# Four-stage transformer block on one core: the projections and the output product of the first stage moved to other slots

## The chip, the cores and the metric

The kernel runs on one core of a Trainium2 chip. The metric is device microseconds of one execution; the lower, the better.

## The reference, cut to what matters

X is 16 sequences of 512 tokens with 256 features, in fp32. Four layers follow each other, each with a layer norm before it and a residual sum behind it:

```python
x = x + attn_a(layernorm(x))     # 16 heads of width 64, exact gelu, output product
x = x + ffn(layernorm(x))        # ternary weights, relu, 256 -> 1024 -> 256
x = x + attn_b(layernorm(x))     # 16 heads of width 16, rotary positions, biases
x = x + ffn(layernorm(x))

def attn_a(X):                   # the first stage, the one that the change touches
    Q, K, V = X @ Wq, X @ Wk, X @ Wv             # 256 -> 1024 each, 16 heads of 64
    attn = softmax(Q K^T / sqrt(64))             # 512 x 512 per head
    A = gelu(attn @ V)                           # exact
    return X + A @ Wpost                         # 1024 -> 256
```

## The kernel before, in words

The program has two stages. The first computes attn_a for all 16 sequences; the second does the other three layers. The change touches the first alone, so only that is told here.

**Units and slots.** A sequence has 16 heads, worked on in 8 pairs. A pair takes 4 units, one for each half of the queries (256 rows) and head; so a sequence has 32 units (`UNITS`) and the stage 512. Every engine walks the same list of *slots*, one for each unit, and in each slot does a fixed set of things, in the order in which its own loop names them. Nothing but semaphores ties the engines together. Slots are counted here from the first of a sequence (slot 0) to 31; slot -1 of a sequence is slot 31 of the one before. In slot u:

- **PE** computes the scores of unit u+3 (`a_scores`, lines L627 and L628, 4 matmuls of 512 columns into half of `ps_s`, which holds two units), then turns the normalised exponentials of unit u (`a_transposes`, L640, two banks of 4 transposes each), then, in every fourth slot (0, 4, 8 and so on: *the values' slots*), the values of the pair that is complete (`a_values`, L656, 32 matmuls), and last the slot's *products* from the table below.
- **ACT** first copies the high part of the products that PE did in the slot before (`a_high`; L837 for q and k), then one turned bank (L824), then takes the exponentials of unit u+3 (L815, two halves, with sums). In slots 19 and 35 (which is slot 3 of the next sequence) it then runs four gelus (L847).
- **DVE** inverts the sums of unit u+2 (L994), then does the low part or copy of the products of the slot before (`a_low`; L1012 for q and k), then the maxima of unit u+3 (L987), then copies the other turned bank (L1001), and behind these the rarer work: the values' copy (L1030, slots 1, 5, 9 ...), the high parts of the gelu results (L1036, slots 4, 5, 20, 21), the statistics (slots 15 to 17) and the normalised rows of the next sequence (`a_normalise`, L982, slots 19 and 20).
- **POOL** multiplies the exponentials of unit u+2 by the inverse of their sums (L535), and computes the low parts of the gelu results (L539).
- **SP** issues the six DMAs that build the stacked q and k of a pair (`a_stack`), in slots -6, -2, 2, 6 and so on; they must have landed before PE computes the first scores of that pair, three slots later.

**Products.** A product is a group of matmuls into one of three PSUM banks: kind "x" is the turned normalised input (two of them, L668), "qk" the projection of a pair to q (i=0) or k (i=1) (six matmuls of 512 columns, L222), "v" the projection of 128 tokens to half of the values (six matmuls, L229), "post" the output product of two blocks of 128 tokens with half of the heads (24 matmuls of 256 columns, L687). They are called Q, V, P and X below.

**Banks.** The two turned banks of each slot and every product are *fills*, numbered in the order of PE's work; fill f goes into bank f mod 3. PE begins a fill only when fill f-3 has been emptied. The first turned bank of a slot is emptied by DVE, the second by ACT; Q and k's product by ACT and then DVE; P by DVE; V by DVE or ACT by the table `value_copy` (of the eight, numbers 0 and 2 of the first half and number 2 of the second go to ACT).

**The tables** that set the slots stand in the lines that the diff shows. Before, the products of pair p stand in slots 4p-8 and 4p-7 (of which the first is a values' slot).

Of the kernel before, what the change touches and what calls it, by code (L numbers as in the profile page):

```python
# [13 lines left out]
def hybrid_block_kernel(nc, X, WQ, WK, WV, WPOST, WB, BQK, BV, WO, BO, W1T, B1, W2T, B2, COS, SIN, X1, OUT):  # L14
# [20 lines left out]
    UNITS = 2 * H  # L35
# [4 lines left out]
    with ctx:  # L40
# [241 lines left out]


        UNITS_ALL = BATCH * UNITS
        XT, QK_FIRST, VALUE_SLOTS = -10, -8, ((-6, -5, -2, -1), (3, 3, 7, 15))
        POST = ((27, 31), (42, 43))
        STATS, AGGREGATE, POWER, NORMALISE = (-17, -16), -15, -15, (-13, -12)
        RESIDUAL, LOAD_X, SAVE_X, STACK_FIRST = 13, -20, 44, -6
        GELUS = (19, 35)
# [7 lines left out]
        def late(s, half):  # L297
            return LATE if (s, half) == (BATCH - 1, 1) else 0

        todo_of = {}  # L300
        for s in range(BATCH):
            for k in range(KT):
                todo_of.setdefault(UNITS * s + XT, []).append(("x", k, 0, s))
            for p in range(PAIRS):
                for i in range(2):
                    todo_of.setdefault(UNITS * s + QK_FIRST + 4 * p + i, []).append(("qk", p, i, s))
            for g in range(2):
                for tok in range(TB):
                    todo_of.setdefault(UNITS * s + VALUE_SLOTS[g][tok], []).append(("v", g, tok, s))
            for half in range(2):  # L310
                for two in range(2):
                    todo_of.setdefault(UNITS * s + POST[half][two] + late(s, half), []).append(("post", half, two, s))

# [951 lines left out]
```

## Time and profile before

| | us |
|---|---|
| median of 3 runs | 4111.77 (4111.37 to 4117.78) |
| profiled execution, its own time | 4113.93 |
| its span | 4112.1 |
| PE busy in the span | 3803.7 (92%) |
| DVE busy | 2600.6 (63%) |
| ACT busy | 2378.7 (58%) |
| POOL busy | 1927.9 (47%) |

The span is what the hardware profiler records from the first to the last instruction; 1.8 us lie around it. PE counts matmuls alone; its weight loads run beside them. The first stage's slots with all their work run from 53.7 us (slot 0 of the first sequence) to about 2341 us; the rest is the second stage.

### The profile page before, as it was taken

The page shows a single profiled execution, that of the slowest core. Times are in us where ns is not written, and L with a number is a line of the kernel's source. Part 1 is how long each engine was busy: PE and PEld are TensorE (multiplying, and loading weights), DVE is VectorE, ACT ScalarE, POOL GpSimd, SP SyncE. Part 2 cuts the span into 40 slices and gives each one's busy share as a digit, 9 for nine tenths or more (in the row PEclk, how much of TensorE's full clock was granted, in tenths as well). Part 3 has the DMA queues.
Part 4 walks back from the last instruction along what each step waited for, and adds up shares of the span by engine and source line. Part 5 has one row for each costly group of instructions (what it writes and reads, how often), then busy time and mean ns, then how long its engine had stood idle before and what let it go on. Part 6 is the DMA issues. An engine that isn't in the chain of part 4 may idle for free.

```text
span 4112.1 us, 65455 instructions
## 1 busy us (share of the span) xinstructions
PE 3803.7 (92%) x23682; PEld 2697.8 (66%) x23682; DVE 2600.6 (63%) x4143; ACT 2378.7 (58%) x4593; POOL 1927.9 (47%) x1219
## 2 busy tenths in 40 slices
PE   6999999999999999999999878999999999999987
PEld 4777777777777777777777654555555555555544
DVE  5665666666566666656656656666666666666662
ACT  3565655556565555655656535666666666666654
POOL 2554455555445455544545543444444444444412
PEclk9999999999999999999999978999999999999998
DMA  4444344344344334444434423232222222322220
GB/s 112 93 103 97 84 103 103 80 101 103 88 93 103 92 88 103 95 96 93 99 92 93 112 49 50 51 55 53 52 53 53 54 52 54 55 54 50 50 42 16
DMA packets 152368, 315.59 MB, mean 77 GB/s; under 512 B 23088, under 2 KB 76720, under 8 KB 152048
## 3 DMA queue, kind: packets, MB, share of 16 engines
q1 hardware_dynamic: 152048, 311.39, 35.3%
q8 instruction: 192, 3.15, 0.3%
q14 instruction: 128, 1.05, 0.1%
HBM read 33.43 MB, written 25.17 MB: 14 GB/s over the span
## 4 chain that ended last, share of the span: by engine, by line
PE 55%; DVE 20%; ACT 13%; issue 7%; POOL 3%; DMA 0%; SPq 0%; DVEq 0%; POOLq 0%; ACTq 0%
PE ps_o L656 10%; DVE neg_max L987 7%; ACT e_a L815 5%; PE ps_o L728 5%; PE ps_t L222 4%; DVE max_b L1128 4%; PE ps_t L764 4%; PE ps_s L701 3%; ACT raw_a L837 3%; PE ps_t L687 3%; PE ps_t L229 3%; PE ps_t L755 3%; PE ps_t L640 3%; PE ps_m L222 2%; DVE xn L1106 2%
## 5 line engine op out<-in xcount | busy, mean ns | idle before, releaser
L535 POOL TENSOR_TENSOR e_a<-e_a,recip 128x1024 f32<-128x1024 f32 x512 | 969.5, 1894 | 1045.1 <-DVE recip L994 1045.1
L815 ACT ACTIVATE e_a<-ps_s,neg_max 128x512 f32<-128x512 f32 x1024 | 693.9, 684 | 249.6 <-DVE neg_max L987 238.7
L853 ACT ACTIVATE et<-ps_s 128x1024 f32<-128x1024 f32 x512 | 523.6, 1023 | 432.9 <-PE ps_s L715 432.8
L1128 DVE TENSOR_REDUCE max_b<-ps_s 128x2 f32<-128x1024 f32 x512 | 623.9, 1219 | 209.3 <-PE ps_s L701 208.0
L987 DVE TENSOR_REDUCE neg_max<-ps_s 128x2 f32<-128x1024 f32 x512 | 621.1, 1213 | 25.3 <-PE ps_s L628 25.3
L656 PE MATMUL ps_o<-et_a,v_a 128*64 128x256 f32 x4096 | 470.3, 382 | 0.0
L640 PE MATMUL ps_t<-ident,e_a 128*128 128x128 f32 x2736 | 394.6, 275 | 41.9 <-DVE et_a L1001 35.8
L627 PE MATMUL ps_s<-stack_a 128*128 128x512 f32 x1024 | 413.0, 403 | 12.9 <-DMA stack_a<-raw_a 8.6
L569 POOL TENSOR_TENSOR h_lo<-h,h_hi 128x512 fp32r<-128x512 f32 x256 | 329.2, 1300 | 180.0 <-ACT h_hi L897 180.0
L628 PE MATMUL ps_s<-stack_a 128*128 128x512 f32 x1024 | 402.4, 393 | 0.0
L640 PEld LDWEIGHTS ps_t<-ident,e_a 128*128 128x128 f32 x2736 | 321.2, 141 | 110.7 <-DVE et_a L1001 51.8
L656 PEld LDWEIGHTS ps_o<-et_a,v_a 128*64 128x64 f32 x4096 | 282.7, 137 | 150.8 <-issue 21.3
L824 ACT ACTIVATE et_a<-ps_t 128x512 f32<-128x512 f32 x339 | 202.2, 596 | 297.5 <-PE ps_t L640 297.3
L994 DVE RECIPROCAL recip<-sums 128x2 f32<-128x2 f32 x512 | 84.8, 166 | 401.4 <-ACT e_a L815 401.4
L701 PE MATMUL ps_s<-k_stack,q_stack 48*128 48x512 f32 x1024 | 261.1, 506 | 68.6 <-DVE max_b L1128 68.1
L557 POOL TENSOR_TENSOR rstd<-rstd,minus_half 128x4 f32<-128x4 f32 x48 | 49.3, 1027 | 499.2 <-DVE rstd L1099 497.6
L728 PE MATMUL ps_o<-et,v_b 128*32 128x512 f32 x2048 | 280.4, 620 | 0.0
L1012 DVE SCALAR_TENSOR_TENSOR raw_a<-ps_t,raw_a 128x512 fp32r<-128x512 f32 x171 | 118.3, 692 | 244.1 <-ACT raw_a L837 242.8
L701 PEld LDWEIGHTS ps_s<-k_stack,q_stack 48*128 48x128 f32 x1024 | 98.4, 187 | 217.5 <-issue 121.8
L1001 DVE COPY et_a<-ps_t 128x512 f32<-128x512 f32 x345 | 234.9, 681 | 0.0
L627 PEld LDWEIGHTS ps_s<-stack_a 128*128 128x128 f32 x1024 | 193.1, 189 | 56.4 <-DMA stack_a<-raw_a 11.6
L640 PE MATMUL ps_m<-ident,e_a 128*128 128x128 f32 x1360 | 206.8, 275 | 19.2 <-DVE et_a L1001 16.8
(207 smaller groups left out, 7965.1 us busy)
## 6 DMA issues: line engine op xcount, KB each, us to landing
stack_a<-raw_a SPq DMA_DIRECT2D x256, 384.0 KB, 4.7
stack_a<-raw_a SPq DMA_DIRECT2D x256, 256.0 KB, 4.3
stack_a<-raw_a SPq DMA_DIRECT2D x256, 128.0 KB, 3.6
q_stack<-roped_q SPq DMA_DIRECT2D x256, 64.0 KB
k_stack<-roped_k SPq DMA_DIRECT2D x256, 64.0 KB
x_a<-X SPq DMA_DIRECT2D x16, 512.0 KB, 3.5
X<-x_a SPq DMA_DIRECT2D x16, 512.0 KB, 3.0
x_ahead<-X SPq DMA_DIRECT2D x16, 512.0 KB, 3.8
```

The source lines that it names most:

```text
L535: nc.gpsimd.tensor_tensor(e_a[:, u % 4, :, :], e_a[:, u % 4, :, :], factor, ALU.mult).then_inc(e_normed, 1)
L569: nc.gpsimd.tensor_tensor(h_lo[:, i, :], h32[:, n % 4, :], h_hi[:, i, :], ALU.subtract).then_inc(h_split, 1)
L627: mm(out, st[:, 0, c:c + P], st[:, 1, :], start=True, stop=False)
L628: last = mm(out, st[:, 0, c:c + P], st[:, 2, :], start=False, stop=True)
L640: last = nc.tensor.transpose(bank(fill)[:, c:c + P], e_a[:, u % 4, j, t * P:(t + 1) * P], ident[:, :])
L656: last = mm(ps_o[HA * h:HA * (h + 1), half * HS:(half + 1) * HS], v_a[:, t, c:c + HA], et_a[:, (4 * n + 2 * half + h) % 5, t, :], start=(t ...
L701: last = mm(ps_s[:, score_bank(u) + h, :], q_stack[rows, pair, block_ * P:(block_ + 1) * P], k_stack[rows, pair, :], start=True, stop=True)
L728: last = mm(ps_o[32 * h:32 * (h + 1), :], v_b[:, s % 2, keys, 4 * quad + h, :], et[:, (2 * w + h // 2) % 5, h % 2, :], start=(keys == 0), ...
L815: ins = nc.scalar.activation(e_a[:, u % 4, j, :], ps_s[:, 2 * (u % 2) + j, :], ACT.Exp, bias=neg_max[:, u % 4, j:j + 1], accum_out=sums[:, ...
L853: nc.scalar.activation(et[:, v % 5, :, :], ps_s[:, 2:4, :], ACT.Exp)\
L987: nc.vector.reduce_max(neg_max[:, u % 4, :], ps_s[:, 2 * (u % 2):2 * (u % 2) + 2, :], AX.X, negate=True)\
L1128: nc.vector.reduce_max(max_b[:, u // 4 % 2, :, u % 4], ps_s[:, score_bank(u):score_bank(u) + 2, :], AX.X, negate=True).then_inc(max_done, 1)
```

## The change

Four tables of slots are written anew; the names, the number of products and what each computes stay.

| | before | after |
|---|---|---|
| Q of pair p (i=0, i=1) | 4p-8, 4p-7 | 4p-9, 4p-7 |
| V, first half of the heads | -6, -5, -2, -1 | -7, -5, -1, 2 |
| V, second half | 3, 3, 7, 15 | 2, 6, 14, 18 |
| P, first half of the heads | 27, 31 | 26, 30 |
| P, second half | 42, 43 (10, 11 of the next) | the same |
| X | -10 | the same |

So the products by slot of a sequence in the midst of the stage (slots 24 to 31 hold products of the next one):

| slots | before | after |
|---|---|---|
| 0 to 3 | Q, Q, none, V V | none, Q, V V, Q |
| 4 to 7 | Q, Q, none, V | none, Q, V, Q |
| 8 to 11 | Q, Q, P, P | none, Q, P, P Q |
| 12 to 15 | Q, Q, none, V | none, Q, V, Q |
| 16 to 19 | Q, Q, none, none | none, Q, V, Q |
| 20 to 23 | Q, Q, X X, none | none, Q, X X, Q |
| 24 to 27 | Q, Q, V, P V | none, Q V, P, Q V |
| 28 to 31 | Q, Q, V, P V | none, Q, P, Q V |

```diff
-        XT, QK_FIRST, VALUE_SLOTS = -10, -8, ((-6, -5, -2, -1), (3, 3, 7, 15))
-        POST = ((27, 31), (42, 43))
+        XT, QK_SLOTS, VALUE_SLOTS = -10, (-9, -7), ((-7, -5, -1, 2), (2, 6, 14, 18))
+        POST = ((26, 30), (42, 43))
...
             for p in range(PAIRS):
                 for i in range(2):
-                    todo_of.setdefault(UNITS * s + QK_FIRST + 4 * p + i, []).append(("qk", p, i, s))
+                    todo_of.setdefault(UNITS * s + QK_SLOTS[i] + 4 * p, []).append(("qk", p, i, s))
```

PE's rows of slot 14 and of the first half of slot 15, before (L627 and L628 are the scores, L640 the turned exponentials):

```order
L627 MATMUL ps_s<-stack_a 128x512
L628 MATMUL ps_s<-stack_a 128x512
L627 MATMUL ps_s<-stack_a 128x512
L628 MATMUL ps_s<-stack_a 128x512
L640 MATMUL ps_t<-ident,e_a 128x128 x4
L640 MATMUL ps_m<-ident,e_a 128x128 x4
L627 MATMUL ps_s<-stack_a 128x512
L628 MATMUL ps_s<-stack_a 128x512
L627 MATMUL ps_s<-stack_a 128x512
L628 MATMUL ps_s<-stack_a 128x512
L640 MATMUL ps_t<-ident,e_a 128x128 x8
```

and now:

```order
L627 MATMUL ps_s<-stack_a 128x512
L628 MATMUL ps_s<-stack_a 128x512
L627 MATMUL ps_s<-stack_a 128x512
L628 MATMUL ps_s<-stack_a 128x512
L640 MATMUL ps_t<-ident,e_a 128x128 x8
L229 MATMUL ps_m<-wa_hi,xh_a 128x512
L229 MATMUL ps_m<-wa_lo,xh_a 128x512
L229 MATMUL ps_m<-wa_hi,xh_a 128x512
L229 MATMUL ps_m<-wa_lo,xh_a 128x512
L229 MATMUL ps_m<-wa_hi,xl_a 128x512 x2
L627 MATMUL ps_s<-stack_a 128x512
```

Slot 14, which held no product, has a V now; behind it PE goes on to the scores of slot 15.

ACT's rows around the four gelus of slot 19, before, from the exponentials of slot 19 to those of slot 20 and the copy behind them:

```order
L815 ACTIVATE e_a,sums<-ps_s,neg_max 128x512 x2
L847 ACT_TABLE_LOAD
L847 ACTIVATE heads_a<-heads_a 128x512 x4
L824 ACTIVATE et_a<-ps_m 128x512
L815 ACT_TABLE_LOAD
L815 ACTIVATE e_a,sums<-ps_s,neg_max 128x512 x2
L837 ACTIVATE raw_a<-ps_t 128x512
```

and now:

```order
L815 ACTIVATE e_a,sums<-ps_s,neg_max 128x512 x2
L847 ACT_TABLE_LOAD
L847 ACTIVATE heads_a<-heads_a 128x512 x4
L837 ACTIVATE raw_a<-ps_t 128x512
L824 ACTIVATE et_a<-ps_t 128x512
L815 ACT_TABLE_LOAD
L815 ACTIVATE e_a,sums<-ps_s,neg_max 128x512 x2
```

The high part of a Q (L837) stands right behind the gelus now, ahead of the turned bank and the next exponentials; it stood behind the next exponentials. The same holds around the gelus of slot 3.

## Rows read from the trace of the kernel before

**Rows 1.** The page's first part: busy time of each engine over the span.

```profile
PE 3803.7 (92%) x23682; PEld 2697.8 (66%) x23682; DVE 2600.6 (63%) x4143; ACT 2378.7 (58%) x4593; POOL 1927.9 (47%) x1219
```

**Rows 2.** Windows, each four slots from 0: length, PE, PEld, DVE, ACT, POOL, clock, DMA, GB/s.

```profile
918.08:936.48 18.40, 17.00 (x105) 12.97 (x104) 10.80 (x17) 9.69 (x23) 6.11 (x5) 1.00 0.30 69
936.48:952.47 15.99, 15.35 (x100) 11.91 (x99) 10.69 (x19) 11.71 (x24) 9.93 (x7) 1.00 0.30 64
952.47:972.62 20.15, 19.86 (x142) 16.50 (x140) 11.36 (x19) 10.97 (x27) 10.34 (x7) 1.00 0.55 125
972.62:988.62 16.00, 15.36 (x101) 11.92 (x99) 9.30 (x14) 7.60 (x18) 8.35 (x5) 1.00 0.39 106
988.62:1003.73 15.11, 14.23 (x93) 10.63 (x92) 10.83 (x25) 8.72 (x22) 7.79 (x5) 1.00 0.41 92
1003.73:1022.55 18.82, 15.82 (x101) 11.67 (x101) 14.68 (x26) 14.49 (x30) 12.99 (x8) 1.00 0.47 103
1022.55:1043.09 20.54, 19.96 (x131) 16.03 (x130) 12.24 (x20) 11.57 (x28) 11.15 (x7) 1.00 0.51 115
1043.09:1063.01 19.92, 19.64 (x129) 15.97 (x128) 11.02 (x17) 9.53 (x23) 7.58 (x5) 1.00 0.36 81
```

**Rows 3.** Timeline of PE, slots 0 to 3: start, length, what, [idle before it <- releaser].

```profile
923.57 0.50 PE L222 MATMUL ps_t<-xh_a,wa_hi 128*128 128x512 f32 x1
...
925.06 0.40 PE L627 MATMUL ps_s<-stack_a 128*128 128x512 f32 x1
...
928.23 0.39 PE L627 MATMUL ps_s<-stack_a 128*128 128x512 f32 x1
...
929.94 0.47 PE L627 MATMUL ps_s<-stack_a 128*128 128x512 f32 x1
...
932.19 0.66 PE L640 MATMUL ps_m<-ident,e_a 128*128 128x128 f32 x4 [0.64 <-DVE et_a L1001]
```

**Rows 4.** Timeline of PE in slot 31: a P, begun at the first row, V behind it.

```profile
1058.67 0.36 PE L687 MATMUL ps_t<-wpost_hi,heads_parts 128*128 128x256 f32 x1
...
1061.62 0.40 PE L229 MATMUL ps_m<-wa_hi,xh_a 128*128 128x512 f32 x1
```

**Rows 5.** Timeline of ACT and DVE in slots 1 to 3.

```profile
929.09 0.59 ACT L837 ACTIVATE raw_a<-ps_t 128x512 fp32r<-128x512 f32 x1
...
929.71 0.69 DVE L1012 SCALAR_TENSOR_TENSOR raw_a<-ps_t,raw_a 128x512 fp32r<-128x512 f32 x1 [0.32 <-ACT raw_a L837]
...
930.32 1.22 DVE L987 TENSOR_REDUCE neg_max<-ps_s 128x2 f32<-128x1024 f32 x1
...
931.45 0.68 DVE L1001 COPY et_a<-ps_m 128x512 f32<-128x512 f32 x1
...
933.05 0.17 DVE L994 RECIPROCAL recip<-sums 128x2 f32<-128x2 f32 x1 [0.92 <-ACT e_a L815]
933.13 1.20 DVE L987 TENSOR_REDUCE neg_max<-ps_s 128x2 f32<-128x1024 f32 x1
```

**Rows 6.** Timeline of ACT and DVE around the gelus of slot 19.

```profile
1005.51 0.81 DVE L982 TENSOR_SCALAR xn_a<-x_a,mean_var,rstd 128x256 f32<-128x256 f32 x2
...
1006.28 0.20 ACT L815 ACTIVATION_READ_ACCUMULATOR e_a<-ps_s,neg_max 128x1 f32 x1
1006.50 1.28 ACT L847 ACT_TABLE_LOAD   x1
...
1009.01 1.53 POOL L539 TENSOR_TENSOR heads_parts<-heads_a,heads_parts 128x512 fp32r<-128x512 f32 x1 [0.36 <-DVE heads_parts L1036]
1009.32 1.70 DVE L982 TENSOR_SCALAR xn_a<-x_a,mean_var,rstd 128x256 f32<-128x256 f32 x2
...
1009.89 0.58 ACT L824 ACTIVATE et_a<-ps_m 128x512 f32<-128x512 f32 x1
1010.48 1.28 ACT L815 ACT_TABLE_LOAD   x1
```

**Rows 7.** SP's last DMA of one pair's stack, and time to landing of such DMAs.

```profile
934.82 0.60 SPq L412 DMA_DIRECT2D stack_a<-raw_a  x1
...
DMA to landing us min/median/max: 4.3/4.7/5.9
```

## The prediction

> **What bounds the kernel now.** I read the page first: PE is busy for 92% of the span, the next engine for 63% [rows 1]. That says that the order of PE's work and its holes matter, not where the holes are. So I cut one sequence in the midst of the first stage into its eight groups of four slots [rows 2]. They add up to 144.9 us, at a full clock; I take this sequence for all of the stage. PE is busy in 137.2 of them. The busy time hides part of the loss, since the matmuls' ends are modelled; the timeline tells it better [rows 3, 4]. From scores to scores a slot without a product takes 1.71 us (928.23 to 929.94), one with a Q 3.17 (925.06 to 928.23): a Q is 1.46, and so is a V. A P is 2.95 (1058.67 to 1061.62). A values' slot up to its product is 5.49 (918.08 to 923.57). An X is four transposes, about 0.45. The first scores behind values cost 0.1 more, a second product of a slot 0.06 less. One values' slot and three slots with a Q or V make 15.1; the eight groups with all the products make **133.2 us**. So PE stands still for 11.7 us a sequence, which is what a better order could get back: over some 15.5 sequences (of the last, only the slots up to 22 hold everything) 181 us.
>
> What it stands still for is shown in slot 3 [rows 3]: a turned bank waits for DVE's copy. Behind that is a loop between DVE and ACT [rows 5]. Call M the start of a slot's maxima (930.32). DVE's turned copy begins 1.13 later and is done at M+1.81; PE begins at M+1.87 (932.19). ACT's exponentials end, and the inverse starts, at M+2.73 (933.05); the next maxima at M+2.81 (933.13) when there is nothing to empty. When a Q is to be emptied, ACT's high part starts 0.10 before the inverse could, DVE's low part 0.62 later, the maxima 0.61 behind that: M+3.83. A V emptied by DVE takes M+3.42, one emptied by ACT leaves it at M+2.81. Before, two slots in a row need 3.83 and then comes a slot in which PE has only 1.71 us of work: PE runs into the loop's lag. Maxima also can't start before the slot's scores, 1.1 behind its start (1.2 behind values).
>
> **The change, group by group.** The number of instructions stays but for some that join or part; nothing is added. The sum is a matter of waits alone, so for each group I take the floor from above and add the waits that the loop's times give.
>
> *Slots 12 to 15.* Count from the start of slot 1 of a group (13 here). The values' slot of 5.49 lets the loop catch up, so M=1.20. Its Q is emptied at 1.20+2.60+0.62+0.69 = 5.11. PE reaches the V of the next slot at 3.26+1.71 = 4.97, but that V needs the bank of the Q: it waits until 5.17, 0.2. The V is emptied by ACT, in time. 15.1+0.2 = **15.3**, before 16.0 [rows 2].
>
> *Slots 16 to 19.* The same, but DVE empties the V: M is 5.03, the copy is done at 5.03+2.81+0.69 = 8.53, PE can go on at 8.59, and the Q in slot 19 would start at 8.34: another 0.25. **15.55**, before 15.1, with two products more in it than before (V and the second Q), where slot 20's left.
>
> *Slots 8 to 11, 24 to 27, 28 to 31.* A P is long enough to let the loop catch up; only the wait on the Q stays (none in 24 to 27, where a V stands between). 19.5+0.2, 19.4 and 18.0+0.2: **19.7, 19.4, 18.2**, before 20.15, 20.5, 19.9.
>
> *Slots 0 to 3.* 15.1+1.46 for the second V, 0.2 for the first, and 0.27 for the second, whose bank is slot 2's turned one (M+1.87 = 6.90, PE there at 6.63): **17.0**, before 18.4.
>
> *Slots 4 to 7.* Here the change has a price. The gelus of slot 3 take ACT for 3.4 us (table load at 1006.50, next work at 1009.89 [rows 6]). The high part of slot 3's Q now stands behind them; before, slot 3 had only V's, emptied by DVE. Count from slot 4: exponentials of slot 3 end at 0.64, the high part starts at 4.05, M is 5.28, the load of the exponentials' table (1.28) ends at 6.5, the inverse comes at 8.0, not 4.9. Slot 5's second turned bank waits for M+1.87, 0.2; slot 6's V for slot 5's Q, whose low part DVE can only finish at 12.1 (high parts of the gelus and the values' copy stand ahead of it) while PE is there at 10.8: 1.3; then 0.1 and 0.25. **17.0**, before 16.0.
>
> *Slots 20 to 23.* The same with the gelus of slot 19: the high part starts at 4.5, M is 5.7. Then DVE has the second pair of normalised rows to make, 1.70 where the first pair took 0.81 [rows 6], so that slot 21's M is 10.2. Waits follow: 0.7 and 1.75 on turned banks in 21 and 22, 1.35 of the first X on slot 21's Q, 1.3 of the second X, 0.5 in slot 23. 14.5+5.6 = **20.15**, before 18.8.
>
> *The sum.* 17.0+17.0+19.7+15.3+15.55+20.15+19.4+18.2 = 142.3, 2.6 less than 144.9; by 15.5, **41 us**. The profiled execution took 4113.9 us; less 41 is 4073. The median of the runs lies 2 us below that execution, so the forecast is 4072. Cover and costs: DVE, ACT and POOL have room (11.0 and 9.5 of 19.9 us in the last group [rows 2]); POOL's work starts behind the inverse and has two slots until PE wants it. The second stage is left as it is.
>
> *The second pair of rows.* It ran 1.70 while POOL ran its 1.53 low part, begun 0.31 earlier [rows 6]; POOL's low part follows the same DVE instruction now, so I take 1.70. Taken at 0.81, the group would be 0.9 shorter and the time 14 us. The Trainium skill (SBUF — State Buffer, "SBUF: two separate sides") says that VectorE in a two-port mode and GpSimd share one pair of ports under an exclusive lock, the one that begins first keeping it. By that rule the 1.70 stays, as in the row.
>
> **The unknown: SP's transfers.** A stack's last DMA is issued at 934.82, 4.4 behind the end of the low part (930.40), and lands 4.3 to 5.9 later, mostly 4.7 [rows 7]: 9.1 to 10.3 in all. Before, the shortest way to the first scores holds a bare slot, two longer ones and the values with a Q. Now it is 15.55-5.11 = 10.4, or 15.3-5.11 = 10.2. Lower bound of its cost: nothing. Upper: 0.4 in each of six groups. I take nothing, as most landings are near 4.7.
>
> **Rivals.**
>
> 1. *The banks come free earlier* (0.13). For it: the waits of 0.2 and 0.25 are differences of long chains, and a tenth less in each halves them; the gelu groups may cost as before. Gone: 1.4 of small waits and half of the 2.4 lost in the gelu groups, together 2.5 a sequence, 39 us more: **4033**.
> 2. *Scores wait for the stack* (0.11), a wait in place of the one removed. It decides once the way from the low part to landing passes 10.2. At 0.3 to 0.4 in five or six groups it takes back 1.5 to 2.2 a sequence: **4095 to 4106**.
> 3. *Slower: the Q behind the gelus* (0.14). Place: slots 4 and 20. Outside of 4 to 7 and 20 to 23 I count a gain of 5.0, within them a loss of 2.4. The change loses once these two groups cost over 5.0 more than before. If the lag that a gelu leaves isn't worked off in the next values' slot but carried on, 8 to 11 and 24 to 27 lose their gains (1.6) and the two groups cost 1.2 each on top: 5.0-1.6-4.8 = -1.4 a sequence, **4134**. Against it: 5.49 of values against a loop of 3.83 works off 1.6.
> 4. *ACT stands still at each table switch* (0.02). Then high parts behind the gelus come later by that time, twice a sequence. The rows show nothing of it: the first load starts 0.02 behind the accumulator read of 1006.28 to 1006.48, the second 0.01 behind the copy of 1009.89 to 1010.47 [rows 6]. An idle time of 1.4 would cost 2 x 1.4 x 15.5 = 43 us: **4115**. The Trainium skill (ScalarE: Activation LUTs, "What ACT_TABLE_LOAD costs") gives 1380 ns of drain beside the 1283 ns load and so speaks against this change; by the rows only the load is there.
>
> **How the numbers follow.** My forecast has 0.60, with a range of its own from 4055 to 4090 (each small wait 0.1 either way, the gelu groups 0.5). A measurement tells 0.2%, 8 us, from no change. Faster by more than that: 0.60+0.13 and 0.04 of rival 2, 0.77. Within it: the other 0.07 of rival 2 and rival 4, 0.09. Slower: rival 3, 0.14. The range runs from rival 1 to the upper bound of rival 2 and to rival 4, 4030 to 4116; rival 3 lies outside, and a little below.
>
> **What would show it.** Groups of four slots, cut as above: 12 to 15 near 15.3 with one wait on L1012 ahead of L229; 0 to 3 near 17; 4 to 7 and 20 to 23 *longer* than before, with waits of over 1 us on L1012 ahead of L229 and L668, and DVE idle for L837 behind the gelus. No wait of 0.64 on L1001 in slots 7, 15, 19. It is wrong if L627 waits for a DMA, if 8 to 11 or 24 to 27 grow, or if the first X doesn't wait.

## The result, and the profile after

The changed kernel takes **4135.7 us** (median of 4 runs, 4133.6 to 4138.8), the one before 4111.6 beside it: ratio 1.0055, 95% interval 1.0043 to 1.0068. It is slower by 0.4 to 0.7%; forecast were 4072 and a range up to 4116.

The page of the kernel after: the span, the busy times, and the granted clock in 40 slices.

```profile
span 4131.8 us, 65455 instructions
PE 3835.5 (93%) x23682; PEld 2731.3 (66%) x23682; DVE 2634.5 (64%) x4143; ACT 2364.6 (57%) x4593; POOL 1929.1 (47%) x1219
PEclk9999999999999999999999978999999999999998
```

The row of the clock reads the same as in the kernel before, digit for digit: a slice is 103 us long, too coarse for what follows. Its mean over the span does differ, 0.984 before and 0.974 now. And PE is busy for 32 us *more* with the same 23682 matmuls [rows 1]. More busy time for the same work means slower matmuls, and the windows show where. One sequence cut as in [rows 2] (length, PE, PEld, DVE, ACT, POOL, clock, DMA, GB/s):

```profile
924.21:941.39 17.18, 17.03 (x106) 13.01 (x104) 10.85 (x16) 8.19 (x21) 7.22 (x4) 1.00 0.34 77
941.39:959.58 18.19, 15.99 (x100) 11.90 (x99) 12.41 (x20) 13.28 (x29) 11.78 (x8) 1.00 0.31 65
959.58:979.40 19.82, 19.75 (x141) 16.57 (x140) 11.46 (x19) 10.01 (x26) 10.49 (x6) 1.00 0.52 120
979.40:994.89 15.49, 15.41 (x100) 11.96 (x98) 9.69 (x15) 8.79 (x22) 8.03 (x5) 1.00 0.45 120
994.89:1010.61 15.72, 15.65 (x100) 11.99 (x98) 11.61 (x25) 8.73 (x22) 8.60 (x6) 1.00 0.45 102
1010.61:1032.93 22.32, 18.27 (x101) 13.80 (x100) 15.27 (x26) 15.19 (x33) 12.67 (x8) 0.85 0.46 105
1032.93:1052.36 19.43, 19.43 (x129) 15.94 (x128) 10.81 (x18) 10.25 (x26) 7.94 (x5) 1.00 0.37 84
1052.36:1070.73 18.37, 18.29 (x123) 14.84 (x122) 11.09 (x18) 8.84 (x22) 7.58 (x5) 1.00 0.36 81
```

| slots | before | forecast | after, this sequence |
|---|---|---|---|
| 0 to 3 | 18.40 | 17.0 | 17.18 |
| 4 to 7 | 15.99 | 17.0 | 18.19 |
| 8 to 11 | 20.15 | 19.7 | 19.82 |
| 12 to 15 | 16.00 | 15.3 | 15.49 |
| 16 to 19 | 15.11 | 15.55 | 15.72 |
| 20 to 23 | 18.82 | 20.15 | 22.32 |
| 24 to 27 | 20.54 | 19.4 | 19.43 |
| 28 to 31 | 19.92 | 18.2 | 18.37 |
| sum | 144.93 | 142.3 | 146.52 |

The mean of sequences 1 to 13 is 145.95. Six groups came out within 0.2 of the forecast. The gain sits where it was expected; two groups ate it. What happens in slots 4 to 6, by the timeline of POOL, DVE, ACT and PE:

```profile
945.56 0.58 ACT L837 ACTIVATE raw_a<-ps_t 128x512 fp32r<-128x512 f32 x1
946.17 0.69 DVE L1012 SCALAR_TENSOR_TENSOR raw_a<-ps_t,raw_a 128x512 fp32r<-128x512 f32 x1 [3.82 <-ACT raw_a L837]
...
949.00 1.41 POOL L539 TENSOR_TENSOR heads_parts<-heads_a,heads_parts 128x512 fp32r<-128x512 f32 x1 [4.68 <-DVE heads_parts L1036]
...
950.37 1.89 POOL L535 TENSOR_TENSOR e_a<-e_a,recip 128x1024 f32<-128x1024 f32 x1
...
951.91 2.04 DVE L1036 CAST heads_parts<-heads_a 128x512 fp32r<-128x512 f32 x2
...
952.23 1.44 POOL L539 TENSOR_TENSOR heads_parts<-heads_a,heads_parts 128x512 fp32r<-128x512 f32 x1
...
953.95 0.66 DVE L1012 SCALAR_TENSOR_TENSOR raw_a<-ps_t,raw_a 128x512 fp32r<-128x512 f32 x1
...
954.66 0.50 PE L229 MATMUL ps_t<-wa_hi,xh_a 128*128 128x512 f32 x1 [2.06 <-DVE raw_a L1012]
```

DVE is idle for 3.82 us until the Q's high part (L837) has come from behind the gelus, as forecast. But then DVE's two casts (L1036, the high parts of the gelu results) take 2.04 us. In the kernel before, the casts of slot 5 took 0.75, with no POOL instruction beside them. Here POOL's L539 and L535 stand in a row from 949.00 to 953.67, and DVE's casts run into them: they end at 953.95, 0.28 behind the end of POOL's second L539. Behind the casts waits the low part of slot 5's Q, and behind that PE, for 2.06.

Slots 22 and 23, timeline of PE, and then the windows of the two slots in this sequence and of slot 23 in an earlier one:

```profile
1022.35 0.63 PE L640 MATMUL ps_t<-ident,e_a 128*128 128x128 f32 x4 [1.22 <-DVE et_a L1001]
1025.02 0.94 PE L668 MATMUL ps_t<-ident,xn_a 128*128 128x128 f32 x4 [1.61 <-DVE raw_a L1012]
1026.75 1.12 PE L668 MATMUL ps_t<-ident,xn_a 128*128 128x128 f32 x4 [0.79 <-DVE et_a L1001]
1030.93 0.78 PE L222 MATMUL ps_t<-xh_a,wa_hi 128*128 128x512 f32 x1
```

```profile
1020.06:1027.52 7.46, 3.85 (x22) 2.73 (x20) 6.63 (x12) 3.81 (x11) 6.19 (x4) 0.85 0.19 41
1027.52:1032.93 5.41, 5.41 (x20) 4.56 (x19) 3.28 (x5) 2.65 (x7) 3.18 (x3) 0.58 1.01 228
```

```profile
736.48:740.32 3.84, 3.73 (x21) 2.80 (x20) 3.06 (x5) 2.44 (x6) 3.56 (x3) 1.00 1.01 230
```

PE pauses three times in slot 22, 3.6 us of 7.5. In this sequence TensorE's clock falls from 2.4 to 1.2 GHz at 1025.26, behind the first two of the pauses and just after the first X has begun (the granted 0.85 over the 7.46 us of the slot says the same: 2.3 us at half). The second X's four transposes take 1.12 instead of 0.66, slot 23 takes 5.41 at a granted 0.58. In the sequence with slot 23 at 736.48 the clock stayed up, and the same slot took 3.84. In the kernel before, the clock never fell between the first and the last scores of the stage; after the change it fell in 14 places there, 85 us in all, and of the sequences 1 to 14 the eleven with a fall behind slot 22 took 146.1 to 146.6 us each, the three without it 144.5.

### The profile page after: what moved, and what is told of

It reads as the page before. It is cut to its first block, busy times and chain, and to the rows that moved or that the text cites. A ratio compares the mean times of both kernels' runs of the same rounds, so it can differ in the third digit from the quotient of the medians.

```text
span 4131.8 us, 65455 instructions
## 1 busy us (share of the span) xinstructions
PE 3835.5 (93%) x23682; PEld 2731.3 (66%) x23682; DVE 2634.5 (64%) x4143; ACT 2364.6 (57%) x4593; POOL 1929.1 (47%) x1219
## 4 chain that ended last, share of the span: by engine, by line
PE 62%; DVE 18%; ACT 9%; issue 6%; POOL 3%; SPq 1%; DMA 1%; DVEq 0%; ACTq 0%; POOLq 0%
PE ps_o L656 8%; PE ps_t L640 5%; PE ps_o L728 5%; PE ps_t L222 4%; PE ps_s L627 4%; DVE max_b L1128 4%; ACT e_a L815 4%; PE ps_t L764 4%; PE ps_s L628 4%; PE ps_s L701 3%; DVE neg_max L987 3%; PE ps_t L687 3%; PE ps_t L755 3%; PE ps_t L229 3%; PE ps_m L222 2%
## 5 line engine op out<-in xcount | busy, mean ns | idle before, releaser
L535 POOL TENSOR_TENSOR e_a<-e_a,recip 128x1024 f32<-128x1024 f32 x512 | 969.3, 1893 | 966.0 <-DVE recip L994 966.0
L627 PE MATMUL ps_s<-stack_a 128*128 128x512 f32 x1024 | 424.9, 415 | 10.3 <-DMA stack_a<-raw_a 10.3
L640 PE MATMUL ps_t<-ident,e_a 128*128 128x128 f32 x2748 | 396.0, 277 | 26.5 <-DVE et_a L1001 18.5
L628 PE MATMUL ps_s<-stack_a 128*128 128x512 f32 x1024 | 410.0, 400 | 0.0
L640 PEld LDWEIGHTS ps_t<-ident,e_a 128*128 128x128 f32 x2748 | 330.6, 143 | 84.9 <-issue 23.6
L627 PEld LDWEIGHTS ps_s<-stack_a 128*128 128x128 f32 x1024 | 196.7, 192 | 95.3 <-issue 45.4
L539 POOL TENSOR_TENSOR heads_parts<-heads_a,heads_parts 128x512 fp32r<-128x512 f32 x128 | 170.9, 1336 | 150.5 <-DVE heads_parts L1036 150.5
L824 ACT ACTIVATE et_a<-ps_m 128x512 f32<-128x512 f32 x168 | 100.4, 598 | 236.5 <-PE ps_m L640 236.5
L1001 DVE COPY et_a<-ps_t 128x512 f32<-128x512 f32 x343 | 233.2, 680 | 0.0
```

Of the source, the lines that this page charges most:

```text
L535: nc.gpsimd.tensor_tensor(e_a[:, u % 4, :, :], e_a[:, u % 4, :, :], factor, ALU.mult).then_inc(e_normed, 1)
L627: mm(out, st[:, 0, c:c + P], st[:, 1, :], start=True, stop=False)
L628: last = mm(out, st[:, 0, c:c + P], st[:, 2, :], start=False, stop=True)
L640: last = nc.tensor.transpose(bank(fill)[:, c:c + P], e_a[:, u % 4, j, t * P:(t + 1) * P], ident[:, :])
```

## The experiments

All are made from the changed kernel but for one. "Group" is four slots as above, means of sequences 1 to 13. "Half clock" is the time at 1.2 GHz between the first and the last scores of the first stage, in the profiled execution.

**1. The Q of slots 3 and 19 put back into slots 4 and 20.**

```diff
-                    todo_of.setdefault(UNITS * s + QK_SLOTS[i] + 4 * p, []).append(("qk", p, i, s))
+                    todo_of.setdefault(UNITS * s + QK_SLOTS[i] + 4 * p + (1 if i == 0 and p % 4 == 3 else 0), []).append(("qk", p, i, s))
```

> The changed kernel, but the Q of slots 3 and 19 stands in the values' slots 4 and 20, as before the change; nothing else moves. Theory A (the Q's high part behind the gelus is what slots 4 to 7 and 20 to 23 lose by): slot 5's M comes no later than before the change, the wait of slot 6's V (2.07 us) falls under 0.8, that of the first X in slot 22 under 1.2, and the clock stays full in the first stage; 2.5 to 4.5 us a sequence less, 4066 to 4097 us. Rival B (DVE's casts and rows, run against POOL, are what is lost, wherever the Q stands): casts of 2.0 and 1.6 us in slots 5 and 21 stay, the waits stay above 1.5, and the time is within 15 us of the changed kernel's 4135.7.

Measured: **4077.5 us**, ratio to the kernel before 0.9912 (0.9899 to 0.9926): 58 us less than the changed kernel, and less than the kernel before. Its windows for slots 0 to 3, 4 to 7, 16 to 19 and 20 to 23:

```profile
903.47:919.19 15.72, 15.57 (x100) 11.80 (x98) 9.62 (x15) 7.01 (x17) 7.22 (x4) 1.00 0.30 63
919.19:938.15 18.96, 17.39 (x107) 13.22 (x106) 12.68 (x22) 14.57 (x30) 11.79 (x8) 1.00 0.38 84
...
973.43:987.45 14.02, 13.96 (x94) 10.75 (x92) 9.98 (x23) 7.77 (x21) 7.14 (x6) 1.00 0.40 93
987.45:1008.02 20.57, 17.47 (x109) 12.87 (x107) 16.32 (x28) 15.71 (x32) 14.36 (x9) 1.00 0.47 107
```

Each pair of groups has the same work as before the edit: 34.7 us for 0 to 7 (35.4 changed), 34.6 for 16 to 23 (37.5, the mean, changed). The clock fell once, for 3.4 us. The casts are at 0.76 to 0.95 too: without the late Q, DVE reaches them before POOL is in the way. So theory A is right about the place, and rival B's casts turn out to be a *consequence* of the lag, not a thing apart.

**2. The gelus one slot later.**

```diff
-        GELUS = (19, 35)
-        HEADS_HIGH, HEADS_LOW = ((20, 20, 21, 21), (36, 36, 37, 37)), ((20, 21, 22, 23), (36, 37, 38, 39))
+        GELUS = (20, 36)
+        HEADS_HIGH, HEADS_LOW = ((21, 21, 22, 22), (37, 37, 38, 38)), ((21, 22, 23, 24), (37, 38, 39, 40))
```

> The changed kernel with the gelus one slot later, in the values' slots 4 and 20 instead of 3 and 19, and the high and low parts of their results one slot later too; no Q is emptied right behind them, and they lie beside 3.6 us of values on PE. Theory A: groups 4 to 7 and 20 to 23 lose at least 1.5 us each, no half clock in the first stage; 3 to 6 us a sequence less, 4043 to 4090 us. Rival B (collisions with POOL are the loss): the casts now stand in slots 5, 6 and 21, 22 and still run 1.6 to 2.0 instead of 0.75; the groups stay as long and the time is 4120 to 4145. Rival C (it only moves the lag): slot 5's M is still late, since ACT needs 3.4 us for the gelus ahead of slot 5's exponentials, and slot 6's V waits more than 1.5 us; 4125 to 4150.

Measured: **4094.6 us**, 0.9957 (0.9944 to 0.9971). Groups 4 to 7 at 17.6 and 20 to 23 at 19.9, casts at 1.16 and 1.19. That is 2.5 us a sequence, short of theory A's least of 3 (and of its 4090 by 5 us); half clock remains (15 falls, 51 us, where theory A said none), and 4 to 7 gained only 0.6, not 1.5. Part of rival C is true: slot 6 still takes 5.3 us, and its V waits 1.87.

**3. The next sequence's rows one slot earlier.**

```diff
-        STATS, AGGREGATE, POWER, NORMALISE = (-17, -16), -15, -15, (-13, -12)
+        STATS, AGGREGATE, POWER, NORMALISE = (-17, -16), -15, -15, (-14, -13)
```

> The changed kernel with the normalised rows of the next sequence one slot earlier (slots 18 and 19 instead of 19 and 20), so that DVE has no rows to make behind slot 20's maxima. Theory A with the rows as its second part: slot 21's maxima start at about 8.6 behind slot 20's start instead of 9.8, the waits of slot 22 (1.2, 1.6, 0.8) shrink by 1 to 2 us together, PE's pause there is shorter and the clock falls in fewer than half of the 11 sequences that show it; 1.5 to 3.5 us a sequence, 4081 to 4112 us. Rival (the casts and POOL set slot 22 anyway): under 0.5 us a sequence, the half clock stays; 4128 to 4136. Groups 4 to 7 stay at 18.2 in either.

Measured: **4123.2 us**, 1.0023 (1.0013 to 1.0033), 12.5 less than the changed kernel; both expectations missed. The rows fall from 1.71 to 0.73, slot 22 from 7.4 to 6.6; but the casts of slot 21 now take 2.05 instead of 1.58, so DVE's time went from one instruction to the next, and the half clock stays (20 falls, 89 us).

**4. POOL's low parts two slots later.**

```diff
-        HEADS_HIGH, HEADS_LOW = ((20, 20, 21, 21), (36, 36, 37, 37)), ((20, 21, 22, 23), (36, 37, 38, 39))
+        HEADS_HIGH, HEADS_LOW = ((20, 20, 21, 21), (36, 36, 37, 37)), ((22, 23, 24, 25), (38, 39, 40, 41))
```

> The changed kernel with POOL's low parts of the gelu results two slots later (slots 6 to 9 and 22 to 25 instead of 4 to 7 and 20 to 23), so that they don't run beside DVE's casts and rows. Theory B (DVE and POOL hold each other up): the rows of slot 20 take 0.8 instead of 1.71 us, the casts of slot 5 at most 1.2 instead of 2.04 and those of slot 21 at most 1.0 instead of 1.59; slot 6's V waits 1.2 instead of 2.07, slot 22 loses 1.5 less, fewer half clocks; 2.5 to 4 us a sequence, 4074 to 4097 us. Rival (the long casts have another cause, such as POOL's multiply, which stays): casts as long as now, under 0.5 us a sequence. A new wait could come: the P of slot 26 needs the low part of slot 25; if PE waits there, up to 1 us a sequence is given back.

Measured: **4071.9 us**, 0.9899 (0.9886 to 0.9913), 64 us less than the changed kernel and 2 us below the range of theory B. All of the casts from 600 to 2000 us, in the changed kernel (the first line) and in this one (the second); min, median and max in ns:

```profile
L1036 DVE CAST heads_parts<-heads_a x76: 412/420/1485, 657.9 to 1973.7; 128x512 fp32r<-128x512 f32 x76
```

```profile
L1036 DVE CAST heads_parts<-heads_a x80: 412/419/425, 642.6 to 1990.2; 128x512 fp32r<-128x512 f32 x80
...
994.92 0.73 DVE L982 TENSOR_SCALAR xn_a<-x_a,mean_var,rstd 128x256 f32<-128x256 f32 x2
...
918.79:935.85 17.06, 15.99 (x100) 11.89 (x98) 11.22 (x20) 13.28 (x28) 9.01 (x6) 1.00 0.33 69
...
986.84:1005.58 18.74, 15.94 (x102) 11.55 (x101) 13.35 (x26) 14.62 (x31) 10.06 (x6) 1.00 0.44 102
```

No cast is long any more, the rows are at 0.73, slots 4 to 7 take 17.06 and 20 to 23 18.74 (the last two lines), slot 6's V waits 0.94 in place of 2.06, and the clock fell twice, 10 us in all. Between 600 and 2000 us no P waits for its low part; the last P of the stage waits 5.97 for it, where it waited 2.57. Nothing but POOL's low parts was moved, so DVE's long casts and rows come from what POOL does beside them: theory B holds, together with A. The Trainium skill (SBUF — State Buffer, "SBUF: two separate sides") describes just such an exclusive lock on a shared pair of ports. The trace agrees: a cast takes 0.42 us alone and up to 1.49 beside POOL, and in the changed kernel all 49 casts of over 0.6 us end 0.28 to 0.29 us behind the end of a POOL instruction.

**5. PE fed in slot 22.**

```diff
+                    if kind == "x" and s:
+                        if a == 0:
+                            pe.wait_ge(a_copied, PAIRS * (s - 1) + 5)
+                        for _ in range((6, 3)[a]):
+                            mm(ps_o[:, :], wa_hi[:, 0, 0:P], wa_lo[:, 0, 0:S], start=True, stop=True)
```

> The changed kernel, but PE runs nine matmuls of 512 columns more in each slot 22 (six ahead of the first X, three ahead of the second, on the weights, into the bank of the values that has been copied out and is written anew in slot 24; their results are not used). They take 9 x 0.23 = 2.1 us of the 2.45 us that PE pauses there, and nothing else waits for them. Theory (the clock halves because PE pauses in slot 22, and 11 of 15 sequences lose 1.6 to 2.1 us by it): the clock stays full in the first stage, the sequences all take about 144.5 us, 4110 to 4120 us. Rival (the half clock has nothing to do with the pause, or costs nothing): as many half clocks as now, 4132 to 4150 us.

Measured: **4121.1 us**, 1.0015 (1.0007 to 1.0024). With nine matmuls more a sequence the kernel is 14.5 us *faster* than the changed one. Slots 22 and 23 take 7.12 and 3.84 in every full sequence, which is what they took in the changed kernel where the clock stayed up (7.10 and 3.84), and no fall is left there. But new ones came: in 8 of the sequences 1 to 14 the clock fell about slots 6 and 7, behind the pause of slot 6, for 3.4 us each, and these took 145.8 to 145.9 us where the others took 144.4 to 144.6. Windows of slots 4 to 7 and 20 to 23:

```profile
939.01:958.54 19.53, 17.33 (x99) 13.04 (x98) 12.69 (x20) 13.47 (x31) 12.86 (x8) 0.91 0.36 80
...
1009.52:1029.91 20.39, 18.01 (x110) 13.04 (x109) 15.06 (x26) 14.62 (x31) 12.71 (x8) 1.00 0.40 94
```

So the pause in slot 22 is what lets the clock fall there, shown by filling it alone. Why the pause in slot 6 is followed by a fall in this kernel (and in 3 sequences of experiment 3) and not in the changed one stays open; what can be said is that a pause of this size puts the clock at risk, and which one is hit differs.

**6. Q and V exchanged around the gelus.**

```diff
-                    todo_of.setdefault(UNITS * s + QK_SLOTS[i] + 4 * p, []).append(("qk", p, i, s))
+                    todo_of.setdefault(UNITS * s + QK_SLOTS[i] + 4 * p - (1 if i == 0 and p % 4 == 3 else 0), []).append(("qk", p, i, s))
...
-        XT, QK_SLOTS, VALUE_SLOTS = -10, (-9, -7), ((-7, -5, -1, 2), (2, 6, 14, 18))
+        XT, QK_SLOTS, VALUE_SLOTS = -10, (-9, -7), ((-7, -5, -1, 2), (3, 6, 14, 19))
```

> The changed kernel with Q and V exchanged around the gelus: the Q of slots 3 and 19 in slots 2 and 18, the V of slots 2 (the second one) and 18 in 3 and 19. A V there is emptied by DVE and needs no ACT, so DVE's maxima of slots 4 and 20 no longer wait for the gelus; POOL's low parts stay where they collide. Theory A (Q's high part behind the gelus starts the lag): slot 5 at most 3.4, slot 6's V waits under 1 us, slots 20 to 23 at most 20.5, 2 to 4 us a sequence, 4074 to 4105 us. Rival B (collisions alone set it): groups 4 to 7 and 20 to 23 stay above 17.7 and 21, 4120 to 4140 us.

Measured: **4080.2 us**, 0.9922 (0.9910 to 0.9934), 55 us less than the changed kernel, though the casts still run 1.6 in slots 5 and 21. Windows of slots 4 to 7 and 20 to 23, which have the same work as in the changed kernel:

```profile
923.93:941.07 17.14, 15.63 (x100) 12.00 (x98) 11.85 (x20) 12.97 (x27) 11.63 (x8) 1.00 0.33 69
...
992.46:1010.99 18.53, 15.68 (x101) 12.01 (x100) 15.05 (x26) 14.15 (x30) 12.68 (x8) 1.00 0.43 98
```

18.2 became 17.1 and 21.8 (the mean) 19.2: a V emptied by DVE behind the gelus, in place of a Q that needs ACT, is worth this without any change on POOL. Slots 16 to 19 give 0.4 back (16.12, from 15.75), and the clock still fell 10 times, 34 us in all. Slot 5 falls to 3.3 from 3.65. Theory A holds; the wait of slot 6's V, though, was not under 1 but 1.51.

**7. The exchange and the late low parts together.** The edits of 4 and 6.

> The exchange of Q and V around the gelus together with the low parts two slots later, which alone gave 4072 us. If both losses are separate, groups 4 to 7 fall from 17.1 to 15.3 to 16.2 and 20 to 23 from 18.8 to 17 to 18, 2 to 4 us a sequence below that run: 4010 to 4045 us, less than both kernels. If they are one loss (once POOL is away, DVE finishes before PE comes), 4065 to 4075 us.

Measured: **4060.8 us**, 0.9872 (0.9859 to 0.9885), the lowest but one; 75 us less than the changed kernel, where the two edits alone gave 64 and 55. Groups 16.5 and 18.2, a little above both forecasts. The time lies between the two expected ranges, 4010 to 4045 and 4065 to 4075. Of the 119 us that the two would give if they added up, 44 overlap: they work on one chain, and neither expectation had that.

**8. The late low parts in the kernel before.** The edit of 4 in the kernel before.

> The kernel before with POOL's low parts two slots later, to see whether that shift alone is worth what it gave to the changed kernel (64 us). If the collisions cost only where the change has brought the loop's lag up to them: the rows of slot 20 take 0.8 instead of 1.70, but they lie behind ACT's gelus and nobody waits; within 6 us of the kernel before. If the collisions cost everywhere: 20 to 60 us faster.

Measured: **4119.7 us**, 1.0015 (1.0006 to 1.0023). All eight groups are within 0.03 of [rows 2]; the second pair of rows went from 1.70 to 0.73, and nobody gained. The collision was there before and cost nothing, since ACT's gelus ended later than DVE's rows. The few us more lie outside of the sequences compared (the span has 0.9 more ahead of the first scores and 2.8 more behind the last). The 2.8 fit the stage's last P, which waits 3.5 us longer for POOL's low part; the first line is from the kernel before, the second from this one:

```profile
2393.61 0.36 PE L687 MATMUL ps_t<-wpost_hi,heads_parts 128*128 128x256 f32 x1 [2.47 <-POOL heads_parts L539]
2399.35 0.55 PE L687 MATMUL ps_t<-wpost_hi,heads_parts 128*128 128x256 f32 x1 [5.97 <-POOL heads_parts L539]
```

So the 64 us of experiment 4 are not a gain that both kernels could have: against the fitting kernel, with the same place for the low parts, the new order of Q, V and P is worth 48 us.

**9. Exchange, late low parts and early rows.** The edits of 3, 4 and 6.

> Q and V exchanged around the gelus, the low parts two slots later, and the normalised rows one slot earlier (slots 18 and 19). In the run without the last (4060.8 us) slot 22 still took 5.12 us and slot 23 4.15, where 3.0 and 3.2 are their work alone, and the half clock was seen six times. If DVE's rows of slot 20 still hold up the inverse of slot 21: 0.5 to 1.2 us a sequence less, 4040 to 4055 us, fewer half clocks. If they are hidden by then, as 0.73 us is little: within 4 us of that run; if the rows now hold up slot 19, where the V is emptied: up to 8 us slower.

Measured: **4058.9 us**, 0.9869 (0.9854 to 0.9884): the same as without the rows' move. At 0.73 the rows are hidden, the second case.

**10. The Q in the values' slots and late low parts.** The edits of 1 and 4.

> The Q of slots 3 and 19 back in the values' slots and the low parts two slots later. Each alone took 4077 and 4072 us. If the two work on one and the same loss (the long casts, which were at 0.75 to 0.95 already without the second edit), the sum of both is little more than one: 4062 to 4077 us, with only the rows of slot 20 (1.70 before) shorter. If they are two separate losses, their gains add up: 4010 to 4030 us.

Measured: **4082.1 us**, 0.9918 (0.9904 to 0.9931), not told apart from experiment 1 (0.9912), and above the expected 4062 to 4077. All eight groups are the same as in 1 within 0.02. With the Q away from the gelus the collisions cost nothing: one and the same loss, as the first case had it. The 4.6 us that it takes more than experiment 1 fit the stage's last P again, which waits 5.94 for its low part in place of 2.53.

## Why the prediction was wrong

**Bounds and the loop: right.** PE's waits for the loop of DVE and ACT set the time, and the loop's times (M+1.87, M+2.81, M+3.83) gave six groups within 0.2 and their sum, 105.2, within 0.8. The small waits on a Q ahead of a V were each 0.1 to 0.2 larger than worked out (slot 14 takes 3.52, not 3.37), and with the rest of these six groups that is 0.8 a sequence, 12 us.

**The step that failed first: "slot 6's V for slot 5's Q, whose low part DVE can only finish at 12.1".** It took the two casts ahead of it at 0.75 us, their length where POOL was not beside them. They took 2.04; the low part ended at 13.2 (954.61 less 941.39) and PE, there at 10.8 as worked out, went on at 13.3: 2.4 by the prediction's own count (2.06 of it idle in the trace), not 1.3. The same text charged the 1.70 of the rows to POOL, and then did not ask what POOL would do beside the next DVE instruction of that kind, though it said that the gelus bring it late. That was 1.2 us a sequence in slots 4 to 7 (18.19 against 17.0), 19 us in all. Experiment 4 is the test: with the low parts out of the way slot 6 takes 4.51, which is the forecast wait of 1.3, slots 4 to 7 take 17.06, and the whole kernel 4071.9 us, within 0.1 us of the number forecast for the changed kernel. That the second agrees so closely is partly luck, as 20 to 23 lost their 1.70 as well.

**The step that was missing: the clock.** Slots 20 to 23 were put at 20.15; in the sequence where the clock stayed they took

```profile
719.94:740.32 20.38, 15.94 (x101) 11.55 (x100) 15.05 (x26) 14.62 (x31) 12.68 (x8) 1.00 0.40 93
```

so the waits were summed almost right, though single ones were off by up to 0.5 (those on turned banks in slots 21 and 22 were 0.4 and 1.2, not 0.7 and 1.75). But the text added 5.6 us of waits within 20 us and costed them at their own length. With them came the half clock in 12 of the 15 full sequences, 1.45 us on the mean of 1 to 13 (145.95 against 144.5), 22 us in all. Experiment 5 shows that the pause is the cause. The prediction named no such term: it took the stage to run "at a full clock" and had no price for its loss.

The sum of what was not in the forecast, 12, 19 and 22 us and another 4 from the 0.23 in slots 20 to 23, is 57 of the 61 that lie between a gain of 41 and a loss of 20 in the profiled executions. The rest lies behind the first stage: from the last scores to the end the span went from 1769.8 to 1774.9 us. Of that stretch one P alone was moved, by one slot; the stage's last P begins some 2 us later behind the last scores than before, and the half clock in the stretch is 3.2 us longer. The cause was not tried.

**Rival 3 named the side and the place, not the mechanism.** Its 4134 us is close to 4135.7 by chance: it had the lag carried on into 8 to 11 and 24 to 27, and these groups gained as forecast (19.8 and 19.4). Its threshold is of the right size: the two gelu groups lost 2.2 and 3.0, 5.2 together, while the others gained 4.2. Rival 2 did not happen: between 600 and 2000 us the scores waited for a stack twice, 0.8 us in all. Rival 4 did not either; the table load at 942.17 starts 0.02 behind the accumulator read. The 1380 ns of drain of the Trainium skill (ScalarE: Activation LUTs, "What ACT_TABLE_LOAD costs") would have put the Q's high part at 946.9, and it started at 945.56: the trace does not bear the drain out, before or after. Rival 1 did not come either: the small waits were larger than worked out, not smaller. Two sums of the prediction are off without touching the forecast: rival 1 speaks of halving the small waits but takes all of their 1.4 away (halved, it comes to some 4042 instead of 4033), and the shortest way of a stack is 4.4 + 4.3 = 8.7 us, not 9.1.

## What to carry to other kernels

An order that fills the bottleneck engine's holes also moves the lag of every other engine; work out for each piece moved what stands *ahead* of its emptying on the other engines (here 3.4 us of gelus), and avoid putting there what needs that engine. Price an instruction by what will run beside it, not by its shortest row: DVE's casts were 0.42 us each alone and up to 1.49 beside POOL. And count a pause of a few us on PE twice, once for itself and once for the clock that may fall behind it.

## What the runs showed of the hardware

A collision of DVE and POOL can cost nothing (experiment 8: rows of 1.70 against 0.73, no group changed by more than 0.03 us) or 64 us (experiment 4), the clock's falls included, by whether somebody waits for DVE then. Not all of DVE's work is hit: its 512 copies of turned banks out of PSUM (L1001) took 0.67 to 0.69 us each in the changed kernel, and 164 of them ran beside a POOL instruction, while the long casts and rows, from SBUF to SBUF, ended only 0.15 to 0.29 us behind POOL's. Extra matmuls can make a kernel faster: nine a sequence gave 14.5 us, as they kept TensorE at 2.4 GHz (slot 23 at 3.84 us instead of 4.9 to 5.6 where it fell).
